# Routing by five-number records instead of finished rows, in a graph and mixture-of-experts kernel

## The chip, the cores and the metric

One core of one Trainium2 chip runs the whole kernel. The metric is device time in microseconds from start to end. Lower is better.

## The reference, cut to what matters

N = 12500 nodes with D = 256 features, 212500 edges, 8 experts with hidden width 512, two experts per node:

```
xn = layernorm(x)
x1 = x + gnn(xn, src, dst, edge_weight) + mix(xn)      # edges: weighted sum of neighbours; mix: gated linear attention
x2 = layernorm(x1)
n  = (x2 - mean(x2)) * rsqrt(var(x2) + eps) * gamma + beta
logits = n @ Wr + br;  top two experts per node;  w = softmax of the two logits
out = x1 + sum over the two experts e:  w_e * (gelu(n @ W1[e] + b1[e]) @ W2[e] + b2[e])
```

## The kernel before, in words

Four phases follow each other, with a barrier of all engines between them. Every engine (PE, DVE, ACT, POOL, and SP, which issues loads and stores) has its own program, written out by hand; semaphores order them.

1. **Setup** (`setup_phase`): constants, edge tables, and clearing of the four accumulators `agg`.
2. **Edges** (`edge_phase`): 1664 chunks of 128 edges in 104 groups of 16. PE and DVE make 128 messages, and POOL adds them into one accumulator with an indirect DMA (L818). Beside the edges, `take_steps` slips in the layer norm of x (the first 25 groups, `normal_steps`), the attention context and the mix; SP stores x + mix as `scratch["x1"]` (L667).
3. **Routing** (`route_phase`): 49 pairs of 128-node tiles. SP loads the four accumulators and x + mix four pairs ahead (`DEPTH = 4`). DVE adds accumulators two and two (`add_halves`, L1629), PE sums and turns them (L1773) and multiplies by the GNN weight (L1784), and DVE adds the result to x + mix, which gives x1 (`gather_sums`, L1623); SP stores x1 to `out`. DVE takes mean and variance (`statistics`) and writes the normalised row into `z` (`normalise`, L1655 and L1657), which has 259 numbers: 256 features, node number, first expert, lead of the first logit over the second. PE turns `z`, ACT applies gamma and beta (`features`), PE makes logits (L1806). DVE picks two experts (`route`) and, with counts that PE makes (L1817 to L1824), each copy's place in its expert's region of a table in DRAM (`position`). POOL scatters each row of `z` twice, with four indirect DMAs a pair (`send`, L1597). At the end SP and ACT write 256 blank rows behind each expert's last row (`fill_up`, L1546), and DVE plans 105 blocks of 256 rows (`plan`).

   The order of one pair on DVE is `route(i-2)`, `gather_sums(i)`, `statistics(i)`, `add_halves(i+2)`, `normalise(i)`, `position(i-2)`. On PE it is `turn(i-1)`, `weigh(i+1)`, `rank(i-2)`, `logits(i-1)`, `sum_turned(i+2)`. On ACT it is `features(i-1)`, the square root for i, `sum_out(i+2)`.
4. **Experts** (`expert_phase`): 105 blocks q, two buffers each. SP loads the block's first-layer weights (L1944) and its 256 rows of the table into `zin` (L1950). PE does the first layer (L1979), turns the next block (L1966), does the second layer (L1989); ACT does gamma, beta and gelu. DVE works out the node numbers and each row's share, adds the bias (L2046) and multiplies by the share (L2052). POOL adds the 256 result rows into `out`, which already holds x1, with two indirect DMAs (L2069). Two copies of one node may stand in neighbouring blocks, so POOL waits until the adds of block q-1 have landed before it issues those of block q:

```
for c in range(2):
    if s == 1:
        pool.wait_ge(s_add[0][c], 16 * k + 16)
    elif not first(k):
        pool.wait_ge(s_add[1][c], 16 * k)
```

## Time and profile before

| what | us |
|---|---|
| median of 3 runs (4436.13 to 4442.04) | 4440.78 |
| the profiled execution | 4440.3 |
| its span in the trace | 4438.6 |
| setup, up to the first add of edges | 0 to about 157 |
| edges | to 3260.9 |
| routing, with its end and the barrier | 3261.0 to 3645.8 |
| experts | 3645.8 to 4438.6 |

In the rows further down, a time at the start of a line counts from the span's start. "Idle before" is the time that an engine stood still before an instruction, with what ended it. Two instructions of one kind in a row overlap a little, so what a pair costs its engine is the distance from its start to the start of the next instruction.

### The profile page before, as it was taken

To read this page: it belongs to the slowest core of one execution; us is meant where nothing else is said; L and a number is where in the kernel's file an instruction comes from. 1 tells how busy PE (TensorE), PEld (TensorE's weight loads), DVE (VectorE), ACT (ScalarE), POOL (GpSimd) and SP (SyncE) were. 2 spreads that over 40 slices of the span, in tenths; PEclk is the share of its full clock that TensorE was granted. 3 is DMA by queue.
4 is the path that set the end of the run, shared out by engine and by line. 5 is a ranking of instruction groups with operands and counts; after the bars stand their busy time and mean duration, and the time that the engine had idled before them with its cause. 6 is when DMAs were issued, how large, how long until landed. Compare 5 with 4: busy or idle time off the path is not lost. (4 is left out here: it accounts for less than half of the span.)

```text
span 4438.6 us, 85552 instructions
## 1 busy us (share of the span) xinstructions
PE 3389.3 (76%) x16628; PEld 2802.7 (63%) x16629; DVE 2495.7 (56%) x11386; ACT 1685.6 (38%) x3095; POOL 3111.7 (70%) x2088
## 2 busy tenths in 40 slices
PE   1466666667677677878888888888758859999998
PEld 1355555555565555666666666666557758888887
DVE  3577777665555555666666666666548862222222
ACT  1233333344444443444444444444312224444443
POOL 0488888888888888888888888888855544444444
PEclk7788878788888888888888888888779979999999
DMA  9888888877777777777777777777789965565554
GB/s 380 241 146 155 152 148 147 157 117 118 116 109 115 116 113 114 102 108 108 105 104 107 108 103 105 108 107 102 91 217 296 294 187 143 139 145 141 141 140 114
DMA packets 588869, 638.95 MB, mean 144 GB/s; under 512 B 60524, under 2 KB 553156, under 8 KB 587138
## 3 DMA queue, kind: packets, MB, share of 16 engines
q0 software_dynamic: 279264, 269.84, 48.5%
q1 hardware_dynamic: 262234, 273.19, 20.9%
q10 hardware_dynamic: 47304, 95.18, 5.9%
q8 instruction: 23, 0.38, 0.0%
q14 instruction: 44, 0.36, 0.0%
HBM read 249.82 MB, written 390.09 MB: 144 GB/s over the span
## 5 line engine op out<-in xcount | busy, mean ns | idle before, releaser
L818 POOL DMA_INDIRECT agg<-msg,sidx x1664 | 2585.7, 1554 | 667.5 <-issue 408.7
L1122 PE MATMUL bank<-rows,Cmat 128*128 x3328 | 1025.7, 450 | 166.7 <-ACT msg L1315 140.6
L1315 ACT COPY msg<-bank 128x512 f32<-128x512 f32 x832 | 487.1, 585 | 1486.0 <-DMA agg<-msg,sidx 1209.8
L1122 PEld LDWEIGHTS bank<-rows,Cmat 128*128 128x128 f32 x3328 | 699.1, 224 | 346.7 <-issue 253.8
L873 DVE SCALAR_TENSOR_TENSOR sidx<-seen_sum,trash,srcf 128x4 int32<-128x4 f32 x416 | 92.7, 223 | 1022.8 <-DMA agg<-msg,sidx 1017.6
L2069 POOL DMA_INDIRECT out_dram<-x_y,x_node x210 | 325.7, 1551 | 473.1 <-issue 228.2
L856 DVE TENSOR_SCALAR Emat<-bank,srcf,wtf 128x128 f32<-128x128 f32 x1664 | 564.5, 398 | 0.0
L1106 PEld LDWEIGHTS bank<-Emat,pick 128*128 128x128 f32 x3328 | 518.3, 226 | 41.6 <-issue 17.7
L1106 PE MATMUL bank<-Emat,pick 128*128 128x128 f32 x3328 | 528.7, 311 | 1.6 <-DVE seen L860 1.6
L1097 PE MATMUL bank<-packed,both 128*128 (+1 forms) x416 | 187.3, 451 | 437.9 <-DVE seen L860 427.9
L860 DVE SCALAR_TENSOR_TENSOR seen<-bank,srcf,prior 128x128 f32<-128x128 f32 x1664 | 479.1, 341 | 0.0
L848 DVE TENSOR_SCALAR pick<-iotaf,locf 128x128 f32<-128x128 f32 x1664 | 384.3, 313 | 13.4 <-issue 12.6
L1097 PEld LDWEIGHTS bank<-packed,both 128*128 (+1 forms) x416 | 47.8, 115 | 530.6 <-issue 408.4
L1979 PE MATMUL bank<-x_xf,x_w 128*128 128x256 f32 x1680 | 381.6, 380 | 1.2 <-ACT x_xf L2005 1.2
L1989 PE MATMUL bank<-expert_rows,x_hT 128*128 x1680 | 380.0, 379 | 0.0
L2021 ACT ACTIVATE x_hT<-bank,ffn_b 128x256 f32<-128x256 f32 x420 | 199.2, 474 | 448.0 <-PE bank L1979 448.0
L1979 PEld LDWEIGHTS bank<-x_xf,x_w 128*128 128x128 f32 x1680 | 320.4, 191 | 45.4 <-issue 1.6
L2046 DVE TENSOR_TENSOR x_y<-bank,expert_rows 128x256 f32<-128x256 f32 x210 | 79.4, 419 | 464.1 <-PE bank L1989 464.1
L1989 PEld LDWEIGHTS bank<-expert_rows,x_hT 128*128 128x128 f32 x1680 | 311.1, 190 | 38.0
L1597 POOL DMA_INDIRECT table<-r_z,r_pos x196 | 197.5, 1008 | 174.5 <-DVE r_pos L1707 112.4
L1306 ACT COPY Cmat<-bank 128x512 f32<-128x512 f32 x416 | 245.3, 590 | 186.0 <-PE bank L1106 184.6
L1321 ACT ACT_TABLE_LOAD x148 | 189.9, 1283 | 7.1 <-SPq L630 4.5
(245 smaller groups left out, 4130.6 us busy)
## 6 DMA issues: line engine op xcount, KB each, us to landing
x_w<-in_L_ffn_W_dram SPq DMA_DIRECT2D x105, 512.0 KB, 4.1
agg<-expert_rows ACTq DMA_DIRECT2D x12, 4224.0 KB, 63.3
r_agg<-agg SPq DMA_DIRECT2D x196, 256.0 KB
x_zin<-table SPq DMA_DIRECT2D x105, 259.0 KB, 4.1
window_raw<-in_x_dram SPq DMA_DIRECT2D x208, 128.0 KB, 2.5
agg<-msg,sidx POOLq DMA_INDIRECT x1664
xn_rows<-n_xn ACTq DMA_DIRECT2D x49, 256.0 KB
xn_turned<-n_xnT ACTq DMA_DIRECT2D x49, 256.0 KB
```

What stands on the lines that cost most here:

```text
L818: pool.indirect_dma_start(scratch["agg"][r][:, :], bass.IndirectOffsetOnAxis(ap=sidx[:, j:j + 1], axis=0), msg[:, j % (2 * BATCH), :], Non ...
L848: nc.vector.tensor_scalar(pick[:, b % 2, q, :], edges["iota"][:], locf[:, bass.ds(BATCH * nb + q, 1)], None, ALU.is_equal)
L856: nc.vector.tensor_scalar(Emat[:, b % 2, q, :], B[b % 2][:, q * P:(q + 1) * P], srcf[:, n], wtf[:, n], ALU.is_equal, ALU.mult)
L860: last = nc.vector.scalar_tensor_tensor(out=seen[:, q, :], in0=B[b % 2][:, q * P:(q + 1) * P], scalar=srcf[:, bass.ds(BATCH * nb + q, 1)], ...
L1097: nc.tensor.matmul(B[b % 2][:, :], edges["both"][:, bass.ds(NB * (g % per) + b, 1)].to_broadcast([P, P]), edges["packed"][:, bass.ds(g // ...
L1106: mm = nc.tensor.matmul(C[:, q * P:(q + 1) * P], pick[:, b % 2, q, :], Emat[:, b % 2, q, :], start=True, stop=True)
L1122: mm = nc.tensor.matmul(M[p][:, (q % 2) * D:(q % 2 + 1) * D], Cmat[:, b % 2, q, :], rows[:, bass.ds(slot, 1), :], start=True, stop=True)
L1306: nc.scalar.copy(Cmat[:, b % 2].rearrange("p q c -> p (q c)"), C[:, :]).then_inc(s_Cc, 1)
L1315: nc.scalar.copy(msg[:, at:at + 2, :].rearrange("p q c -> p (q c)"), M[p][:, :]).then_inc(s_msg, 1)
L1979: mm = nc.tensor.matmul(H[c][:, 0:CAP], w1[:, s, a, c * P:(c + 1) * P], xf[:, s, a, :], start=(a == 0), stop=(a == HALF - 1))
L1989: mm = nc.tensor.matmul(Y[s][:, h * D:(h + 1) * D], hT[:, s, c, h * P:(h + 1) * P], w2[:, bass.ds(e * HC + c, 1), :], start=(c == 0 and h ...
L2069: pool.indirect_dma_start(out[:, :], bass.IndirectOffsetOnAxis(ap=node[:, s, c:c + 1], axis=0), y[:, s, c, :], None, bounds_check=N - 1, o ...
```

## The change

- The table holds records of five numbers: node, first expert, lead, mean, 1/deviation. The routing writes no normalised row. POOL scatters records with the same four indirect DMAs a pair.
- PE turns x1 itself, directly after it is summed. The router's gamma, beta and mean are folded into its weights once, ahead of the loop, and 1/deviation scales the logits afterwards.
- x1 is stored to `scratch["x1"]`. `out` is cleared in the edge phase, by 25 DMAs of 512 KB (the last one smaller) from ACT's queue, one in each of the first 25 groups.
- In the expert phase SP loads a block's records three blocks ahead, DVE turns the node numbers into integers (`tell`), POOL gathers the 256 rows of x1 with two indirect DMAs (`gather`), and DVE normalises them one block ahead (`normalise`). The copy of a node that belongs to its first expert also carries x1 (`own`, `xe`), so that the sums in `out` start at zero. Four slots of records and rows take the place of two of `zin`, and the loop runs over four blocks.

```diff
 def edge_phase
+            def blank_out(n):
...
+                    act.dma_start(out[bass.ds(n * BLANK * P, BLANK * P), :].rearrange("(p a) d -> p (a d)", a=BLANK),
+                                  blank).then_inc(s_blankout, 16)
             def normal_steps(n):
-                steps = [(1, lambda u=u: deviations(n, u)) for u in pairs_of(n)]
+                steps = [(1, lambda u=u: deviations(n, u)) for u in pairs_of(n)] + [(8, lambda: blank_out(n))]
 def route_phase, DVE, statistics(i, u)
                 dve.wait_ge(s_st, 3 * i + 1)
+                if not below(i, DEPTH):
+                    for c in range(2):
+                        for m in range(2):
+                            dve.wait_ge(s_sent[c][m], 16 * (i - DEPTH + 1))
                 dve.nop(nofuse=True)
                 for c in range(2):
-                    last = nc.vector.bn_aggr(mv[:, s, c, :], stat[:, c, :])
+                    last = nc.vector.bn_aggr(rec[:, u, c, MEAN:RSTD + 1], stat[:, c, :])
...
-                nc.vector.reciprocal(scl[:, s], std[:, s]).then_inc(s_scl, 1)
-                dve.wait_ge(s_scl, i + 1)
-                if not below(i, DEPTH):
-                    dve.wait_ge(s_T, i - DEPTH + 1)
-                    for c in range(2):
-                        for m in range(2):
-                            dve.wait_ge(s_sent[c][m], 16 * (i - DEPTH + 1))
-                nc.vector.tensor_copy(z[:, u, :, D], nodes[:, bass.ds(2 * i, 2)])
-                for c in range(2):
-                    last = nc.vector.tensor_scalar(z[:, u, c, 0:D], x1[:, s, c, :], mv[:, s, c, 0:1], scl[:, s, c:c + 1],
-                                                   ALU.subtract, ALU.mult)
-                last.then_inc(s_z, 1)
+                nc.vector.reciprocal(rec[:, u, :, RSTD], std[:, s]).then_inc(s_scl, 1)
+                nc.vector.tensor_copy(rec[:, u, :, NODE], nodes[:, bass.ds(2 * i, 2)])
 route(i, u)
-                nc.vector.tensor_tensor(lg[:], logit, br[:].rearrange("p (a e) -> p a e", a=1).to_broadcast([P, 2, NE]),
-                                        ALU.add).then_inc(s_lg, 1)
+                dve.wait_ge(s_scl, i + 1)
+                for c in range(2):
+                    last = nc.vector.scalar_tensor_tensor(out=lg[:, c, :], in0=logit[:, c, :], scalar=rec[:, u, c, RSTD:RSTD + 1],
+                                                          in1=brc[:], op0=ALU.mult, op1=ALU.add)
 PE, turn(i, u); POOL, send
-                pe.wait_ge(s_z, i + 1)
+                pe.wait_ge(s_sum, i + 1)
-                                                z[:, u, c, :], None).then_inc(s_sent[c][m], 16)
+                                                rec[:, u, c, :], None).then_inc(s_sent[c][m], 16)
 def expert_phase, SP
+            def body(k, u):
+                q, s = SLOTS * k + u, u % 2
                 e = expert_of(sp, q)
-                if not first(k):
+                if not below(q, 2):
                     sp.wait_ge(s_H, HC * (q - 1))
                     sp.nop(nofuse=True)
                 sp.dma_start(w1[:, s], ...)
-                sp.dma_start(zin[:, s], scratch["table"][bass.ds(at, CAP), :].rearrange("(a p) d -> p a d", p=P)).then_inc(s_z[s], 16)
+                if not over(q + AHEAD):
+                    if not below(q, 1):
+                        sp.wait_ge(s_share, q)
+                        sp.nop(nofuse=True)
+                    load_records(*ahead(k, u, AHEAD))
 PE, turn
-                pe.wait_ge(s_z[s], 16 * k + 16)
+                pe.wait_ge(s_zn, q + 1)
 DVE
+            def normalise(k, u):
+                q, s = SLOTS * k + u, u % 2
+                dve.wait_ge(s_gat[u], 32 * k + 32)
...
+                for c in range(2):
+                    last = nc.vector.tensor_scalar(zn[:, s, c, :], xg[:, u, c, :], rec[:, u, c, MEAN:MEAN + 1],
+                                                   rec[:, u, c, RSTD:RSTD + 1], ALU.subtract, ALU.mult)
...
+                    last = nc.vector.tensor_scalar(xe[:, s, c, :], xg[:, u, c, :], own[:, s, c:c + 1], None, ALU.mult)
...
-                    nc.vector.tensor_scalar(y[:, s, c, :], y[:, s, c, :], share[:, s, c:c + 1], None,
-                                            ALU.mult).then_inc(s_y, 1)
+                    nc.vector.scalar_tensor_tensor(out=y[:, s, c, :], in0=y[:, s, c, :], scalar=share[:, s, c:c + 1],
+                                                   in1=xe[:, s, c, :], op0=ALU.mult, op1=ALU.add).then_inc(s_y, 1)
+            def body(k, u):
+                if not over(q + 1):
+                    normalise(*ahead(k, u, 1))
+                if not over(q + AHEAD):
+                    tell(*ahead(k, u, AHEAD))
+                shares(k, u)
+                finish(k, u)
 POOL
+            def gather(k, u):
+                pool.wait_ge(s_row, SLOTS * k + u + 1)
...
+                    pool.indirect_dma_start(xg[:, u, c, :], None, scratch["x1"][0:NPAD, :],
+                                            bass.IndirectOffsetOnAxis(ap=rows[:, u, c:c + 1], axis=0)).then_inc(s_gat[u], 16)
+            def body(k, u):
+                if not over(q + AHEAD):
+                    gather(*ahead(k, u, AHEAD))
```

DVE in the loop of the routing, from the square root's result to the logits, before (`r_std` comes from ACT, `r_sent` counts landed scatters, `r_place`, `run` and `r_pos` belong to `position`, `r_lg` to the next pair's `route`):

```order
L1629 TENSOR_TENSOR r_agg<-r_agg 128x1024 [waits r_sums_loaded0]
L1648 RECIPROCAL r_scl<-r_std 128x2 [waits r_std]
L1654 REGISTER_ALU [waits r_turned,r_scale]
L1655 ISA [waits r_sent10,r_sent11,r_sent01,r_sent00]
L1655 COPY r_z<-nodes 128x2
L1657 TENSOR_SCALAR r_z<-r_x,r_mv,r_scl 128x256 x2
L1695 TENSOR_TENSOR r_place<-bank,run 128x16 [waits r_ranks]
```

The same place with the change, from the statistics on:

```order
L1667 REGISTER_ALU [waits r_stat_step]
L1670 BN_AGGR r_record<-r_stat 128x2 [waits r_sent11,r_sent10,r_sent00,r_sent01]
L1670 BN_AGGR r_record<-r_stat 128x2
L1672 REGISTER_ALU
L1673 TENSOR_SCALAR r_vs<-r_record 128x2 [waits r_stat_step]
L1653 ISA
L1655 TENSOR_TENSOR r_agg<-r_agg 128x1024 [waits r_sums_loaded0]
L1678 RECIPROCAL r_record<-r_std 128x2 [waits r_std]
L1679 ISA
L1679 COPY r_record<-nodes 128x2
L1718 TENSOR_TENSOR r_place<-bank,run 128x16 [waits r_ranks]
```

The two writes of the normalised rows are gone, and the wait for the scatters of four pairs ago has moved from behind the reciprocal to the statistics, about 2 us earlier in the round.

POOL in the loop of the experts, one block before (`x_added` counts landed adds, `x_out_weighted` finished result rows):

```order
L2067 ISA [waits x_added10,x_added11]
L2069 DMA out_dram<-x_y,x_node 12500x256 [waits x_out_weighted]
L2067 REGISTER_ALU
L2069 DMA out_dram<-x_y,x_node 12500x256 [waits x_out_weighted]
L2062 REGISTER_ALU
```

and one block with the change (`x_rows` are the gathered rows, the first of the two names in `x_rows<-x_rows` being the buffer and the second x1 in DRAM):

```order
L2148 DMA x_rows<-x_rows,x_row 128x256 [waits x_rows_told]
L2148 DMA x_rows<-x_rows,x_row 128x256
L2157 ISA
L2160 ISA [waits x_added10,x_added11]
L2162 DMA out_dram<-x_y,x_node 12500x256 [waits x_out_weighted]
L2160 REGISTER_ALU
L2162 DMA out_dram<-x_y,x_node 12500x256 [waits x_out_weighted]
```

Two gathers stand between the adds of one block and the wait for them that precedes the next block's adds.

## Rows read from the trace of the kernel before

**Rows 1.** Stretches: length, PE, PEld, DVE, ACT, POOL busy, PE clock, DMA share, GB/s.

```profile
500.00:700.00 200.00, 134.50 (x611) 109.50 (x611) 147.99 (x675) 62.08 (x130) 167.22 (x108) 0.80 0.85 147
3450.00:3550.00 100.00, 83.11 (x647) 74.30 (x647) 83.63 (x396) 24.68 (x58) 56.44 (x57) 0.95 0.94 294
3664.00:4424.00 760.00, 760.00 (x3725) 669.46 (x3724) 202.79 (x832) 309.72 (x725) 321.04 (x207) 1.00 0.58 140
```

**Rows 2.** A round of routing, DVE and first scatter, timeline: start, duration, instruction.

```profile
3452.16 0.25 DVE L1640 BATCH_NORM_AGGREGATE r_mv<-r_stat 128x2 f32<-128x6 f32 x2
...
3454.25 0.17 DVE L1655 COPY r_z<-nodes 128x2 f32 x1 [0.41 <-DVE r_scl L1648]
3454.33 0.83 DVE L1657 TENSOR_SCALAR r_z<-r_x,r_mv,r_scl 128x256 f32<-128x256 f32 x2
3455.08 0.24 DVE L1695 TENSOR_TENSOR r_place<-bank,run 128x16 f32<-128x16 f32 x2
...
3455.87 0.17 DVE L1707 CAST r_pos<-r_posf 128x4 int32<-128x4 f32 x1
...
3456.90 0.96 POOL L1597 DMA_INDIRECT table<-r_z,r_pos  x1 [2.15 <-DVE r_pos L1707]
```

**Rows 3.** The same round on PE, by the timeline.

```profile
3453.83 2.05 PE L1773 MATMUL bank<-ident,r_agg 128*128 128x128 f32 x16 [0.92 <-DVE r_agg L1629]
...
3458.71 1.04 PE L1806 MATMUL bank<-ffn_wrt,r_xf 128*128 128x8 f32 x8
```

**Rows 4.** Instructions of tile r_x: ns min/median/max, first and last start.

```profile
L1623 DVE TENSOR_TENSOR r_x<-r_xin,bank x49: 686/686/689, 3275.1 to 3611.3; 128x512 f32<-128x512 f32 x49
```

**Rows 5.** Instructions of tile table, the scatters of the routing, and their landing.

```profile
L1597 POOL DMA_INDIRECT table<-r_z,r_pos x196: 957/963/1998, 3292.0 to 3632.8; - x196
...
DMA to landing us min/median/max: 2.9/4.2/8.9
```

**Rows 6.** The end of the routing and the start of the experts, by the timeline.

```profile
3632.82 0.96 POOL L1597 DMA_INDIRECT table<-r_z,r_pos  x1 [1.97 <-DMA table<-r_z,r_pos]
...
3647.78 0.40 SPq L1950 DMA_DIRECT2D x_zin<-table  x1
...
3651.79 1.12 PE L1966 MATMUL bank<-ident,x_zin 128*128 128x128 f32 x4 [30.37 <-DMA x_zin<-table]
```

**Rows 7.** Source line of the barrier behind the routing.

```profile
L1462 POOLq DRAIN  x1: 7084/7084/7084, 3638.6 to 3638.6; - x1
```

**Rows 8.** Adds of the experts on POOL, by the timeline.

```profile
3740.18 1.55 POOL L2069 DMA_INDIRECT out_dram<-x_y,x_node  x1 [3.71 <-DMA out_dram<-x_y,x_node]
3742.04 1.55 POOL L2069 DMA_INDIRECT out_dram<-x_y,x_node  x1 [0.30 <-issue]
3747.83 1.55 POOL L2069 DMA_INDIRECT out_dram<-x_y,x_node  x1 [4.24 <-issue]
...
3754.95 1.55 POOL L2069 DMA_INDIRECT out_dram<-x_y,x_node  x1 [3.72 <-DMA out_dram<-x_y,x_node]
```

**Rows 9.** The adds of the experts (L2069): start to landing, min/median/max.

```profile
DMA to landing us min/median/max: 2.7/4.9/6.2
```

**Rows 10.** One block of the experts on PE and DVE, by the timeline.

```profile
3670.70 3.62 PE L1979 MATMUL bank<-x_xf,x_w 128*128 128x256 f32 x16
3671.03 0.75 DVE L2046 TENSOR_TENSOR x_y<-bank,expert_rows 128x256 f32<-128x256 f32 x2 [5.27 <-PE bank L1989]
3671.82 0.62 DVE L2052 TENSOR_SCALAR x_y<-x_y,x_share 128x256 f32<-128x256 f32 x2
...
3674.16 0.60 PE L1966 MATMUL bank<-ident,x_zin 128*128 128x128 f32 x4
...
3678.05 3.62 PE L1979 MATMUL bank<-x_xf,x_w 128*128 128x256 f32 x16
```

**Rows 11.** Edges: the adds (L818) and DVE's `pick` (L848), by source and tile, 300:3200.

```profile
L818 POOL DMA_INDIRECT agg<-msg,sidx x1558: 1545/1547/1968, 298.9 to 3200.0; - x195
L848 DVE TENSOR_SCALAR pick<-iotaf,locf x1556: 176/281/608, 304.2 to 3194.3; 128x128 f32<-128x128 f32 x195
```

More of the change, by code:

```diff
@@ L54 @@
 ROW = D + 3
+REC = 5
+NODE, FIRST, LEAD, MEAN, RSTD = range(REC)
 TABLE_ROWS = NE * REGION + CAP
@@ L1981, in body @@
                     mm.then_inc(s_H, 1)
-                if not (isinstance(k, int) and q == BLOCKS - 1):
-                    turn(*((k, 1) if s == 0 else (k + 1, 0)))
-                if not first(k):
+                if not over(q + 1):
+                    turn(q + 1, 1 - s)
+                if not below(q, 2):
                     pe.wait_ge(s_yb, q - 1)
@@ L2071, in body @@
                                             compute_op=ALU.add).then_inc(s_add[s][c], 16)
+            for u in range(AHEAD):
+                gather(0, u)
             over_blocks(pool, body)
```

227 lines of the change are left out of this document (140 added, 87 removed).

## The prediction, with its working

> **What bounds the kernel now.** I read the table by stretches first, then one round of each phase in the timeline.
>
> In the edges POOL is the bound: the adds start on average (3200.0 - 298.9) / 1557 = 1.863 us apart, and one takes 1.545 us plus 0.30 us of issue, 1.845 us [rows 8, 11]. Only 0.02 us an add is left for everything else, although the DMA engines are 85% busy [rows 1].
>
> In the routing DVE is. One pair is one round; the 49 sums of x1 start (3611.3 - 3275.1) / 48 = 7.00 us apart [rows 4]. In the round shown DVE stands still only 0.41 us [rows 2]. PE needs from 3453.83 to 3459.75, 5.92 us, for what it does between one sum of accumulators and the next [rows 3], and idles for the rest. POOL needs 4 x (0.96 + 0.30) = 5.04 us. The DMA engines are busy 94% [rows 1], so about 6.6 us of the 7.0, yet no load is what DVE waits for.
>
> In the experts PE is busy 760.00 of 760.00 us at full clock [rows 1]; a block takes 7.35 us [rows 10]. POOL's adds are close behind: three blocks' first adds start 7.65 and 7.12 us apart, 7.39 on average [rows 8]. A block's adds wait for landings, not for results: the result rows of the block before 3674 are ready about 3672.4 [rows 10], while idle times of 3.71 to 4.24 us before the adds end with landings [rows 8].
>
> **The change part by part.**
>
> *Edges.* 25 more DMAs, 12.8 MB in all, go to ACT's queue in the first 25 groups. If no other work hid them, 12.8 MB at the 294 GB/s of the routing [rows 1] are 44 us; that is the upper end. The lower end is 0. I take +1 us: POOL's issue is what counts here, an add has 7.4 us (four adds' spacing) until its accumulator is wanted again, and landings of such adds in the experts have a median of 4.9 us [rows 9]. The cover is POOL's descriptor work; if it were gone, the bytes would show.
>
> *Routing, the round.* DVE loses the two writes of normalised rows, from 3454.33 to 3455.08, 0.75 us, and the stand of 0.41 us ahead of them [rows 2]. The logits are scaled and biased in two instructions where one did it; the pair at 3455.08 takes 0.24 us [rows 2], so against one such instruction 0.1 us more. 7.00 - 0.75 - 0.41 + 0.10 = 5.94 us. PE's 5.92 us stay as they are, since it turns as many tiles; ACT only gets shorter. With both engines at 5.9 and each waiting for the other twice a round I take 6.05 us: 48 x (7.00 - 6.05) = **46 us gained**. POOL's 5.04 us fit. For the DMA engines a pair moves 1.5 MB in place of 2.05, which takes their 6.6 us to about 5. Ends: 5.85 us a round (the last products of PE overlap the next sum), 55 us; 6.4 us, 29 us.
>
> What is late next: the wait for the scatters of four pairs ago, now ahead of the statistics. In the new round it lies 2 T - 2.7 us behind the positions of that pair (two rounds, less the 3.71 us from statistics to positions without the 1.16 us that went, plus 0.17 us of the cast) [rows 2]. The positions, ready at 3456.04, release the first scatter at 3456.90, 0.9 us later [rows 2]; the fourth starts 3.8 us later, and it lands 4.2 us after that at the median [rows 5]: 8.9 us, against 9.4 us at T = 6.05. It fits by half a microsecond.
>
> *Routing, set-up and end.* The folding of weights (four small DVE instructions, eight products, three more) lies in the first microseconds, in which DVE has only the first loads to wait for; +0. At the end the blank rows are 5 KB in place of 259 KB for each of nine DMAs. The last scatter waited 1.97 us where others wait 0.30 [rows 6], and POOL was released at 3638.6 [rows 7], 5.8 us after that scatter's start, where the shortest landing is 2.9 us [rows 5]. Both together give up to 4.6 us; I take **-4**. Then POOL's sequencer drains for 7.1 us [rows 7]. I can't tell from the trace what for, and leave it; that is up to 6 us of downside in the range.
>
> *Experts, the start.* Before, the rows' load is issued at 3647.78 and PE turns them at 3651.79, 4.0 us [rows 6]. Now a chain stands there: records load (between 2.7 and 4.0 us, take 3.3), cast 0.3, first gather 0.3, second gather 1.26 behind it, its landing (2.7 to 6.2 us, take 4.2) [rows 5, 9], normalisation 0.8: 10.2 us, begun about 1 us earlier, by estimate, because no weights load is ahead of it. **+5 us**; ends +3 and +8.
>
> *Experts, the blocks.* PE's work is the same, so 0 as long as nobody makes it wait. The first cover is DVE's: PE turns the next block at 3674.16 [rows 10]. DVE gets the block's products at 3671.03, adds the bias until 3671.82, then weighs and adds x1 (0.62 before; by the pair of 0.75 in rows 2 at most that), then normalises, 0.75: ready about 3673.4, 0.7 us early. DVE's total rises from 202.79 / 760 of 7.35 = 2.0 us a block by about 1.9, to 4. The second cover is POOL's: two gathers of 0.96 + 0.30 = 2.5 us fall into its idle 3.71 to 4.24 us [rows 8]. A gather is not in this trace; its ends are the plain scatter's 0.96 and the add's 1.55 us, and it is a plain copy, so I take 0.96. Even at 1.55 both need 3.7 us and just fit. Should this cover go, every microsecond beyond costs 105 times. SP now waits for a block's shares between two weight loads, but the weights are loaded two blocks ahead; +0. The records' bytes are few, and 256 gathered rows replace 256 loaded ones.
>
> The Trainium skill speaks against this part: "SBUF — State Buffer", section "Who interferes with whom", says that a DVE instruction in a two-port mode, which tensor_scalar on SBUF operands can enter, locks GpSimd out of the port through which it writes descriptors. Four such instructions of 256 columns a block are new here. The trace doesn't agree: beside 1556 `pick` instructions of that form, of 281 ns, the edges' adds take 1547 ns at the median and 1545 at least [rows 11]. By the rule the blocks would be longer; by the rows they are not, and the sum keeps 0. That case is rival B.
>
> **The sum:** -46 - 4 + 5 + 1 = -44 us. 4440.3 - 44 = **4396 us**. The profiled execution's 4440.3 is within 0.5 us of the median 4440.78, so it stands for the median too.
>
> **The rivals.**
>
> *A. The records land too late.* The wait of half a microsecond's spare binds the round: 2 T - 2.7 = 4.7 + landing. With landings of 5.9 us, T = 6.65, a gain of 17 us and 4440 - 17 - 4 + 5 + 1 = **4425**; at 6.6 us T is 7.0 and nothing is left. For: DVE waited at just this wait before, with more time to spare, and landings reach 8.9 us [rows 2, 5]. Against: the engines get a quarter less to move. The Trainium skill ("DMA: Bandwidth & Descriptors", the specifications at its head) says that transfers below 512 bytes are a read-modify-write; the records have 20 bytes. No row here shows a price for it.
>
> *B. The adds become the bound of the experts, and the kernel slower.* The adds' round of 7.39 us is 1.85 us from first to second add and 5.54 us from there to the next block's first, most of it the landing [rows 8, 9]. PE's is 7.35. If gathers in the same queue, or DVE's new instructions, lengthen it, blocks follow it once the lead of some 3 us is used up. From 0.42 us a block on, the whole gain is gone (44 / 105), from 0.5 us the kernel is slower by over 0.2%. Landings longer by 0.8 us give 44 fewer microseconds gained and 80 lost, 4396 + 80 = **4476**. If each of DVE's new instructions from SBUF to SBUF held POOL up for its whole length, the net 0.9 us a block (two pairs of 0.75 less the 0.62 that the weighing took) would give 4396 + 90 = **4486**; that is what the Trainium skill's page "SBUF — State Buffer" would have. For: there is no spare in the chain. Against: the load of 259 KB that now runs at the same time as the adds goes, and landings go down to 2.7 us when loads are absent [rows 9].
>
> *C. The clearing of the output shows.* Half of its bytes on the path are 22 us: **4418**. Against: rows 11.
>
> *D. Better than the sum.* Rounds of 5.85 us, and a shorter drain: 55 + 8 - 4 = 59 us, **4381**.
>
> **How the numbers follow.** Forecast 0.62, A 0.14, B 0.12, C 0.04, D 0.08. 0.2% of the time, 9 us, is about what a measurement of this kernel can tell from no change. Faster by more than that: the forecast, D, nearly all of A and C and a little of B, 0.84. Within it: ends of A, B and C, 0.06. Slower: most of B, 0.10. The range 4376 to 4428 takes in the forecast's ends (rounds of 5.85 to 6.4 us, start +3 to +8, end 0 to -10), D, the middle of A, and C; it leaves out B and the far end of A.
>
> **What would show each step.** Right: sums of x1 about 6.0 us apart with DVE and PE both nearly full; statistics that don't wait for scatters; scatters at 0.96 us; blocks at 7.35 us with PE without gaps; gathers near 0.96 us; the first turn of the experts 9 to 11 us after the first record load; adds of the edges still 1.86 us apart. Wrong: the mean-and-variance instruction waiting for record landings (A); adds in the experts 7.8 us or more apart and PE waiting for the normalised rows (B); adds waiting for landings in the first 25 groups (C).

## The result, and the profile after

| | before | after |
|---|---|---|
| time, median (lowest to highest), us | 4439.55 (4436.13 to 4442.04), 4 runs | 4525.01 (4522.28 to 4529.99), 4 runs |
| ratio to before | | 1.0194, 95% interval 1.0177 to 1.0212 |
| span of the profiled execution, us | 4438.6 | 4528.2 |
| first sum of x1 in the routing | 3275.1 | 3269.1 |
| last sum of x1 | 3611.3 | 3608.5 |
| first add of the experts | 3665.7 | 3663.0 |
| last add of the experts | 4431.0 | 4524.2 |

The change made the kernel slower by 1.9%. The forecast was 4396 us, with a range to 4428: the sign was wrong. The stages say where: up to the first sum of x1 -6.0 us, the 48 rounds of the routing +3.2 (where -46 were forecast), from there to the first add of the experts +0.1, from the first to the last add +95.9 (where 0 was forecast), behind the last add -3.6. Together +89.6 us, the difference of the spans.

The first and the last of these terms lie outside the routing's rounds and the experts' blocks. The -6.0 us do not belong to the change: on another chip the first sums of x1 start at 3273.7 us before it (run before_again) and at 3274.3 us with it (after_again). The -3.6 us are the last drain of POOL's sequencer (source L1888 before, L1915 after), which no term of the forecast has:

```profile
L1888 POOLq DRAIN  x1: 8788/8788/8788, 4429.5 to 4429.5; - x1
```

```profile
L1915 POOLq DRAIN  x1: 5216/5216/5216, 4522.7 to 4522.7; - x1
```

It takes 5.2 us in every run in which POOL gathers among the experts, and 8.8 us in the two kernels that don't (the kernel before and the run x_load).

The stretches of the changed kernel, as in [rows 1] (length, PE, PEld, DVE, ACT, POOL busy, PE clock, DMA share, GB/s):

```profile
500.00:700.00 200.00, 135.50 (x610) 112.34 (x618) 147.66 (x679) 62.92 (x132) 167.05 (x109) 0.81 0.87 167
3450.00:3550.00 100.00, 83.39 (x629) 75.14 (x629) 74.53 (x376) 18.24 (x42) 62.67 (x56) 0.91 0.81 220
3661.00:4421.00 760.00, 702.45 (x3320) 585.51 (x3319) 348.58 (x1288) 278.72 (x645) 482.34 (x365) 1.00 0.57 125
```

In the routing DVE has lost 9 us of work in 100, as intended, and stands still for as much longer. In the experts PE, 760.00 of 760.00 before, is down to 702.45: somebody makes it wait. The rows of the edges (source L825 and L855, 300:3200; [rows 11] before) show nothing of the clearing; the add is even 5 ns shorter, and in the 25 groups with the clearing the adds start 1.86 us apart before and after:

```profile
L825 POOL DMA_INDIRECT agg<-msg,sidx x1562: 1541/1542/1990, 299.1 to 3199.8; - x196
L855 DVE TENSOR_SCALAR pick<-iotaf,locf x1560: 174/282/610, 304.4 to 3194.1; 128x128 f32<-128x128 f32 x195
```

**The routing.** The sums of x1 (tile r_x), the statistics (source L1670) with what ended DVE's idle time ahead of them, and the scatters (source L1612); [rows 2, 4, 5] before:

```profile
L1649 DVE TENSOR_TENSOR r_x<-r_xin,bank x49: 686/689/690, 3269.1 to 3608.5; 128x512 f32<-128x512 f32 x49
...
L1670 DVE BATCH_NORM_AGGREGATE r_record<-r_stat x98: 148/166/185, 3270.7 to 3610.2; 128x2 f32<-128x6 f32 x98
...
  DMA expert_records<-r_record,r_pos: 45.0, 32
...
L1612 POOL DMA_INDIRECT expert_records<-r_record,r_pos x196: 952/958/1974, 3285.9 to 3628.8; - x196
```

(3608.5 - 3269.1) / 48 = 7.07 us a round. The wait that the prediction named as "late next" is there, 32 times, 45.0 us. One of the longer instances, by the timeline:

```profile
3445.59 0.17 DVE L1730 CAST r_pos<-r_posf 128x4 int32<-128x4 f32 x1
3446.62 0.95 POOL L1612 DMA_INDIRECT expert_records<-r_record,r_pos  x1 [1.05 <-DVE r_pos L1730]
...
3450.41 1.46 POOL L1612 DMA_INDIRECT expert_records<-r_record,r_pos  x1 [0.30 <-issue]
...
3457.37 0.25 DVE L1670 BATCH_NORM_AGGREGATE r_record<-r_stat 128x2 f32<-128x6 f32 x2 [2.07 <-DMA expert_records<-r_record,r_pos]
3457.93 1.97 POOL L1612 DMA_INDIRECT expert_records<-r_record,r_pos  x1 [1.53 <-DMA expert_records<-r_record,r_pos]
```

The pair's fourth scatter starts at 3450.41, 4.8 us behind its positions as forecast, but by its semaphore's events it lands at 3457.15, 6.8 us after its start where the working took 4.2. Over the 49 pairs, by the same events (a few per cent of them are missing), the last landing of the four comes 5.6 us after the fourth's start at the median (2.1 to 8.6), and 5.5 us in the kernel before.

The 4.2 us were not a landing of these scatters at all. The line "DMA to landing us min/median/max: 2.9/4.2/8.9" in [rows 5] counts only DMAs on the table whose landing is known, and none of the 196 scatters is among them: they are 105 loads of the experts' rows (source L1950: 3.7/4.1/5.6), 8 stores of blank rows (L1546: 4.2/6.5/8.9) and one more (L1879: 2.9).

**The experts.** Two blocks on POOL, SP (its DMA queue, SPq) and DVE:

```profile
3870.00 1.61 POOL L2162 DMA_INDIRECT out_dram<-x_y,x_node  x1 [1.09 <-issue]
3870.71 0.33 SPq L1986 DMA_DIRECT2D x_record<-expert_records  x1
3871.91 1.65 POOL L2162 DMA_INDIRECT out_dram<-x_y,x_node  x1 [0.30 <-issue]
3872.30 0.39 SPq L1995 DMA_DIRECT2D x_w<-in_L_ffn_W_dram  x1
3873.87 1.01 POOL L2148 DMA_INDIRECT x_rows<-x_rows,x_row  x1 [0.30 <-DMA out_dram<-x_y,x_node]
3875.19 0.99 POOL L2148 DMA_INDIRECT x_rows<-x_rows,x_row  x1 [0.30 <-issue]
3877.34 0.17 DVE L2102 CAST x_node<-x_record 128x2 int32<-128x2 f32 x1 [4.28 <-DMA out_dram<-x_y,x_node]
3878.21 1.63 POOL L2162 DMA_INDIRECT out_dram<-x_y,x_node  x1 [2.03 <-issue]
3880.15 1.68 POOL L2162 DMA_INDIRECT out_dram<-x_y,x_node  x1 [0.30 <-issue]
3880.20 0.38 SPq L1995 DMA_DIRECT2D x_w<-in_L_ffn_W_dram  x1
3881.09 0.66 PE L2017 MATMUL bank<-ident,x_normal 128*128 128x128 f32 x4 [0.57 <-DVE x_normal L2091]
```

The first adds of two blocks are 8.21 us apart; over the stage (4524.2 - 3663.0) / 104.5 = 8.24, against (4431.0 - 3665.7) / 104.5 = 7.32 before (104 distances between first adds, and the last block's second add). From the second add to the next block's first it is 6.30 us here against 5.79 in [rows 8]; over the 96 blocks in mid-stage 6.41 against 5.49. By the landing events the second add lands 3.72 us after its end, against 2.93; the rest of the growth is in the adds themselves, whose second takes 1.68 us where it took 1.55 (medians). The first add lands sooner than before, 3.9 us after its start against 5.6, but the chain waits for the second. PE's idle time is ahead of the turn, behind the normalised rows: DVE normalises the next block only when it is through with the one before, and for that it waits for landed adds (L2102). So everything follows the adds' chain. The gathers last what they were forecast to last, and POOL has room for them.

What SP's queue waits for in the experts, before (3665:4430) and after (3665:4520), by the table of waits:

```profile
SPq L1943 <- PE bank L1979: 449.0, 102, 4.8
```

```profile
SPq L1999 <- DVE x_share L2108: 570.1, 99, 6.4
SPq L2007 <- DMA out_dram<-x_y,x_node: 21.0, 1, 21.0
SPq L1994 <- PE bank L2030: 6.3, 1, 6.3
```

Before, the load of W1 was released by PE. Now its own wait (L1994) ends at once: SP has already been held at the shares (L1999), which DVE works out when adds have landed. So W1, 512 KB, is issued 2.04 us after a block's first add on average, where it was 0.28 us (both from the starts of L1995 and L2162, and of L1944 and L2069, over 96 blocks). By the DMA engines' packets its bytes now move from 3 to 6.5 us after the first add, just when the second add's should (in x_gate below they start at 4 us), and those start at 5 us.

The start of the experts, by the timeline, and the barrier behind the routing (source L1478):

```profile
L1478 POOLq DRAIN  x1: 7084/7084/7084, 3631.2 to 3631.2; - x1
```

```profile
3639.28 2.57 SPq L1986 DMA_DIRECT2D x_record<-expert_records  x3
...
3648.54 1.11 PE L2017 MATMUL bank<-ident,x_normal 128*128 128x128 f32 x4 [30.28 <-DVE x_normal L2091]
```

### The profile page after: what moved, and what is told of

Same layout as the page of the kernel before. It is cut to its first block and busy times, and to the rows that moved or that the text cites. A ratio compares the mean times of both kernels' runs of the same rounds, so it can differ in the third digit from the quotient of the medians.

```text
span 4528.2 us, 86264 instructions
## 1 busy us (share of the span) xinstructions
PE 3396.8 (75%) x16480; PEld 2800.9 (62%) x16637; DVE 2662.7 (59%) x11974; ACT 1665.9 (37%) x3046; POOL 3350.3 (74%) x2298
## 5 line engine op out<-in xcount | busy, mean ns | idle before, releaser
L825 POOL DMA_INDIRECT agg<-msg,sidx x1664 | 2577.2, 1549 | 668.2 <-issue 403.6
L2162 POOL DMA_INDIRECT out_dram<-x_y,x_node x210 | 346.0, 1648 | 262.5 <-issue 241.0
L855 DVE TENSOR_SCALAR pick<-iotaf,locf 128x128 f32<-128x128 f32 x1664 | 385.2, 314 | 14.0 <-issue 13.7
L1104 PE MATMUL bank<-packed,both 128*128 (+1 forms) x260 | 118.0, 454 | 339.8 <-DVE seen L867 329.9
L1612 POOL DMA_INDIRECT expert_records<-r_record,r_pos x196 | 215.1, 1098 | 161.0 <-DVE r_pos L1730 82.2
L2102 DVE CAST x_node<-x_record 128x2 int32<-128x2 f32 x105 | 18.0, 171 | 435.8 <-DMA out_dram<-x_y,x_node 434.5
L2148 POOL DMA_INDIRECT x_rows<-x_rows,x_row x210 | 209.5, 998 | 78.0 <-issue 46.0
```

The source lines that it names most:

```text
L825: pool.indirect_dma_start(scratch["agg"][r][:, :], bass.IndirectOffsetOnAxis(ap=sidx[:, j:j + 1], axis=0), msg[:, j % (2 * BATCH), :], Non ...
L855: nc.vector.tensor_scalar(pick[:, b % 2, q, :], edges["iota"][:], locf[:, bass.ds(BATCH * nb + q, 1)], None, ALU.is_equal)
L2148: pool.indirect_dma_start(xg[:, u, c, :], None, scratch["x1"][0:NPAD, :], bass.IndirectOffsetOnAxis(ap=rows[:, u, c:c + 1], axis=0)).then_ ...
L2162: pool.indirect_dma_start(out[:, :], bass.IndirectOffsetOnAxis(ap=node[:, s, c:c + 1], axis=0), y[:, s, c, :], None, bounds_check=N - 1, o ...
```

## The experiments

The runs of one set share a chip, and chips differ: the kernel before takes 4438 to 4453 us on them, and the changed kernel's routing code, unedited, runs in rounds of 6.9 to 7.5 us. So ratios are to the kernel before on the same chip, and rounds are compared within a set. Even there one code's mean round varies from profile to profile: r_both and all_three have the same routing and differ by 0.24 us. "Round" is the mean distance of the routing's sums of x1, "block" that of the experts' blocks, both from one profile. A ratio without an interval is from one run of each kernel, or of the experiment.

| set | run | ratio | round | block |
|---|---|---|---|---|
| 1 | r_late | 1.021 | 7.34 | 8.22 |
| 1 | x_load | 1.031 | 7.34 | 8.61 |
| 1 | x_narrow | 1.021 | 7.46 | 8.23 |
| 1 | x_relax | 1.000 | 7.40 | 7.32 |
| 2 | r_rank | 1.018 | 7.13 | 8.23 |
| 2 | r_both | 1.018 | 7.09 | 8.23 |
| 2 | x_once | 1.000 | 7.38 | 7.32 |
| 2 | all_three | 0.9994 (0.9984 to 1.0003) | 7.33 | 7.32 |
| 3 | before_again | 1.000 | 7.16 | 7.33 |
| 3 | after_again | 1.0207 (1.0190 to 1.0224) | 7.28 | 8.22 |
| 3 | r_third | 1.023 | 7.46 | 8.21 |
| 3 | x_ahead | 1.017 | 7.19 | 8.05 |
| 4 | x_gate | 0.997 | 6.88 | 7.32 |
| 4 | r_light | 1.018 | 6.95 | 8.22 |
| 4 | r_both_light | 1.016 | 6.60 | 8.25 |
| 4 | gate_both | 0.9946 (0.9929 to 0.9963) | 6.63 | 7.32 |

Runs x_... touch the experts, runs r_... the routing, all_three and gate_both touch both; all edits are made to the changed kernel. x_load, x_narrow, x_once, r_light and r_both_light leave out or replace a part of the work, so their output is not the kernel's; they serve for timing alone.

### Is it the gathers?

x_narrow gathers 64 numbers in place of a row's 256, a quarter of the bytes (NARROW is 64):

```diff
-                    pool.indirect_dma_start(xg[:, u, c, :], None, scratch["x1"][0:NPAD, :],
+                    pool.indirect_dma_start(xg[:, u, c, 0:NARROW], None, scratch["x1"][0:NPAD, :].rearrange("n (a d) -> (n a) d", d=NARROW),
```

> The changed kernel with gathers of 64 numbers of each row in place of 256 (the rest of a row is zero, so the experts' rows are not the right ones). If the adds land late because the gathers' descriptors are written and queued behind them, nothing changes: landing 3.7 us, round 8.3, time about 4525. If it is the gathers' bytes on the DMA engines, landing falls to 3.0 to 3.2 us, round to 7.6, time about 4450.

Block 8.23, nothing changed. The gathers' bytes are not it. x_load has no gathers at all:

```diff
-                    gather(*ahead(k, u, AHEAD))
+                sp.dma_start(xg[:, u], scratch["x1"][bass.ds(64 * (SLOTS * k + u), CAP), :]...).then_inc(s_gat[u], 16)
```

> The changed kernel with the rows of x1 brought by one plain load of 256 rows by SP, in order of rows and not by the records (so the rows that the experts work on are not the right ones), and no gathers on POOL. Theory G (gathers on POOL's queue right behind the adds make the adds land later): landing of the second add after its end falls from 3.7 to about 2.9 us, round of adds from 8.34 to 7.35 to 7.5, time 4435 to 4445. Rival P (the new work of DVE slows the adds themselves and that decides): add's duration stays at 1.63 to 1.68 us, landing stays at 3.7, round about 8.2, time 4510. Rival D (DVE's order, with shares behind normalise and tell, decides): round stays at 8.3.

All three theories missed: the block grew, to 8.61. The gathers are gone and it got worse, so their being gone does not bring the time back; x_once below clears them in full. What came in their place is one more load that SP issues at about the same time as W1, and the second add is further from the next block's first, 6.85 us against 6.41. That pointed to SP's loads.

### Is it the chain of adds, and what lengthens it?

x_relax: the plan adds a tile that holds 16 where the expert changes and 0 elsewhere, and POOL waits by it.

```diff
-                for c in range(2):
-                    if not below(q, 1):
-                        pool.wait_ge(s_add[1 - s][c], 16 * (2 * k + u // 2) + 16 * s)
+                if not below(q, 1):
+                    want = 16 * (2 * k + u // 2) + 16 * s
+                    if not isinstance(k, int):
+                        new = pool.value_load(fresh[0:1, bass.ds(q, 1)], min_val=0, max_val=16)
+                        want = want - 16 + new
+                    for c in range(2):
+                        pool.wait_ge(s_add[1 - s][c], want)
```

> The changed kernel, in which the adds of a block wait for those of the block before only where the expert changes (two blocks of one expert share no node); the adds of two blocks before are still waited for by DVE. Theory: the chain of adds alone makes the round of 8.34 us; without it the experts are bound by PE at 7.35 us again, or DVE's chain at 7.4 to 7.6, time 4430 to 4450. Rival D (DVE's wait for the adds of two blocks before, then shares and finish in one row, is a cycle of its own): round 7.9 to 8.3, time 4480 to 4525.

Block 7.32, as before the change: without the chain of adds the whole loss is gone, and DVE's own order has no cycle that binds. This run alone doesn't say what lengthened the chain, since W1's load moved too: its packets now run 5 to 7.5 us after the first add.

x_once loads W1 for two blocks only:

```diff
-                if not below(q, 2):
-                    sp.wait_ge(s_H, HC * (q - 1))
-                    sp.nop(nofuse=True)
-                sp.dma_start(w1[:, s], ...
+                if below(q, 2):
+                    sp.dma_start(w1[:, s], ...
```

> The changed kernel with W1 loaded for the first two blocks only (all blocks use those weights, so the experts work with the wrong ones), gathers and adds as they are. Theory C (W1's packets, which in the changed kernel run at 3 to 6.5 us of the round of adds, hold up those of the second add): its landing after its end falls from 3.72 to 2.2 to 2.9 us, round of adds from 8.34 to 7.3 to 7.5, ratio to the kernel before 0.995 to 1.003. Rival G (the gathers behind the adds on POOL's queue hold them up, whatever their bytes): landing stays at 3.5 or more, round at 8.1 or more, ratio 1.014 or more.

Block 7.32, with the wait for the block before, the gathers and DVE's new instructions all in place. PE is full again (3700:4400):

```profile
3700.00:4400.00 700.00, 700.00 (x3432) 616.56 (x3431) 343.29 (x1333) 278.55 (x665) 498.53 (x382) 1.00 0.44 71
```

So the chain carries the loss, and W1's load in it makes it. Is it the load's bytes, which were there before the change too, or its time? x_ahead gives W1 four slots, loads a block ahead, and puts the load in front of the records':

```diff
+                if not below(q, 1):
+                    sp.wait_ge(s_share, q)
...
+                if not below(q, 3):
+                    sp.wait_ge(s_H, HC * (q - 2))
...
+                if not over(q + 1):
+                    load_w1(*ahead(k, u, 1))
                 if not over(q + AHEAD):
                     load_records(*ahead(k, u, AHEAD))
```

> The changed kernel with four slots for W1, its load issued one block ahead and in front of the records' load on SP; nothing is left out. Theory C (it is the time at which W1's packets run against those of the second add that costs): they now start up to 2 us earlier in the round of adds, the second add's landing falls from 3.72 to 2.9 to 3.3 us and the block from 8.24 to 7.35 to 7.8, ratio to the kernel before 1.000 to 1.010. Rival (any W1 load beside the adds costs the same wherever it lies, as the bytes are the same): block stays at 8.1 or more, ratio 1.015 or more.

Block 8.05 on average, outside both forecasts, but the average hides two kinds. Two stretches of the same run:

```profile
3905.12 1.61 POOL L2167 DMA_INDIRECT out_dram<-x_y,x_node  x1 [1.21 <-issue]
3906.45 0.37 SPq L1991 DMA_DIRECT2D x_w<-in_L_ffn_W_dram  x1
3907.03 1.59 POOL L2167 DMA_INDIRECT out_dram<-x_y,x_node  x1 [0.30 <-issue]
3912.63 1.62 POOL L2167 DMA_INDIRECT out_dram<-x_y,x_node  x1 [1.39 <-issue]
...
4012.19 1.62 POOL L2167 DMA_INDIRECT out_dram<-x_y,x_node  x1 [2.31 <-issue]
4014.11 1.57 POOL L2167 DMA_INDIRECT out_dram<-x_y,x_node  x1 [0.30 <-issue]
4014.56 0.27 SPq L1991 DMA_DIRECT2D x_w<-in_L_ffn_W_dram  x1
4020.67 1.61 POOL L2167 DMA_INDIRECT out_dram<-x_y,x_node  x1 [2.37 <-issue]
```

Where W1 is issued 1.33 us after the first add, the next block's comes after 7.51 us; where it is 2.37 us, after 8.48. Over 96 blocks: issue before 1.75 us, 25 blocks of 7.5 us; from 2 us on, 53 blocks of 8.4. The 18 blocks between take 8.2 us. The bytes are the same. x_gate takes the step to its end and lets SP issue the load when the adds of three blocks before have landed:

```diff
+                def landed():
+                    if not below(q, 3):
+                        for c in range(2):
+                            sp.wait_ge(s_add[1 - u % 2][c], 16 * (2 * k + (u - 1) // 2))
+                            sp.nop(nofuse=True)
...
+                if not over(q + 1):
+                    load_w1(*ahead(k, u, 1), landed)
+                if not below(q, 1):
+                    sp.wait_ge(s_share, q)
...
```

> As x_ahead, with W1's load issued by SP right when the adds of three blocks before have landed, ahead of its wait for the shares; nothing is left out, and the wait of the adds for the block before stays. In x_ahead the blocks whose W1 load was issued under 1.75 us after the first add took 7.5 us and the others 8.2 to 8.4. Theory C (the time of W1's packets, not their bytes): the issue now falls near the first add's start (within 0.5 us, as in the kernel before, where it is 0.28 us after it), landing of the second add about 2.9 us, block 7.35 to 7.55, ratio to the kernel before 1.000 to 1.007. Rival (the bytes beside the adds cost the same wherever they lie): block 8.1 or more, ratio 1.015 or more.

```profile
3901.85 0.38 SPq L1993 DMA_DIRECT2D x_w<-in_L_ffn_W_dram  x1
3903.29 1.65 POOL L2176 DMA_INDIRECT out_dram<-x_y,x_node  x1 [1.20 <-DVE x_y L2139]
3905.25 1.57 POOL L2176 DMA_INDIRECT out_dram<-x_y,x_node  x1 [0.30 <-issue]
3907.12 1.01 POOL L2162 DMA_INDIRECT x_rows<-x_rows,x_row  x1 [0.30 <-issue]
...
3910.64 1.67 POOL L2176 DMA_INDIRECT out_dram<-x_y,x_node  x1 [1.22 <-DVE x_y L2139]
```

Block 7.32, and a ratio of 0.997, a little better than the forecast of 1.000 to 1.007. The load is issued 1.4 us ahead of the first add, earlier than I had written, the second add lands 2.2 us after its end where 2.9 was expected, and the chain has slack: the first add waits for its result rows (x_y), no longer for landings. The gathers, DVE's new instructions, the load's bytes and the wait for the block before are all still there. Time, not bytes, is shown.

### Why did the routing gain nothing?

r_late keeps mean and 1/sigma in tiles of their own (mv) and copies them into the record two rounds later, behind the wait:

```diff
-                if not below(i, DEPTH):
-                    ... dve.wait_ge(s_sent[c][m], 16 * (i - DEPTH + 1))
-                    last = nc.vector.bn_aggr(rec[:, u, c, MEAN:RSTD + 1], stat[:, c, :])
+                    last = nc.vector.bn_aggr(mv[:, u, c, :], stat[:, c, :])
 route, of the pair two rounds back
+                    ... dve.wait_ge(s_sent[c][m], 16 * (i - DEPTH + 1))
+                nc.vector.tensor_copy(rec[:, u, :, MEAN:RSTD + 1], mv[:, u])
```

> The changed kernel, with mean and 1/sigma kept in a ring of their own and copied into the record two rounds later, so that a slot of records waits for scatters six rounds back, not four. Theory W (the wait at the statistics for the scatters of four pairs before sets the round of 7.07 us): the wait goes from DVE's statistics, rounds fall to 6.1 to 6.4 us, 49 rounds give 33 to 45 us, time about 4480 to 4492. Rival L (the round is bound by loads, turns or the scatters' own chain of four, and the wait only shows it): rounds stay at 6.9 to 7.1 us and the idle time moves to another wait, time 4518 to 4530. Experts' rounds stay at 8.3 us by both.

Round 7.34, within those of untouched routing in the same set (7.34 to 7.46). The wait at the statistics is gone, and in about every second round DVE's position waits for PE's ranks instead (L1721, second row):

```profile
3475.30 0.23 DVE L1721 TENSOR_TENSOR r_place<-bank,run 128x16 f32<-128x16 f32 x2
3483.16 0.26 DVE L1721 TENSOR_TENSOR r_place<-bank,run 128x16 f32<-128x16 f32 x2 [1.37 <-PE bank L1857]
```

A new bound right behind the old. r_rank lifts that one alone, r_both lifts both:

```diff
-                    weigh(i + 1, (u + 1) % DEPTH)
                 if not below(i, 2):
                     rank(i - 2, (u - 2) % DEPTH)
+                if not (isinstance(i, int) and i == PAIRS - 1):
+                    weigh(i + 1, (u + 1) % DEPTH)
```

> The changed kernel, with PE's rank sums of a pair put ahead of the weighing of the next, not behind it. Theory two bounds (the wait for the scatters at the statistics, and behind it a cycle of two rounds in which DVE's position waits for the ranks that PE works out behind the weighing): this edit alone lifts the second only, so rounds stay at 7.1 to 7.4 us and time within 15 us of the changed kernel's (ratio to the kernel before 1.016 to 1.020). Rival (PE's order alone was the bound, and the wait at the statistics was slack): rounds fall to 6.1 to 6.6, ratio 1.008 to 1.012.

> Both edits of the routing together: the late record and the rank sums ahead of the weighing. Theory two bounds: neither wait is left, rounds fall to DVE's own row of 6.3 to 6.6 us, ratio to the kernel before 1.008 to 1.012. Rival (loads at four fifths of the DMA engines, or PE at its lower clock, bound the round whatever the order): rounds stay at 7.1 or more, ratio 1.016 or more.

7.13 and 7.09, against 7.38 in x_once, whose routing is untouched. That is 0.25 to 0.29 us, hardly more than the 0.24 us by which r_both's routing differs from itself in all_three; r_both stands where its rival said (7.1 us, ratio 1.016 or more), not at the forecast 6.3 to 6.6. r_third has the late record and the ranks ahead too, moves the logits ahead of the weighing, turns a pair in its own round instead of the next, and moves ACT's copy to fit:

> The routing with the late record, and PE's round in the order ranks, logits, weighing, turning (of the same pair), sum, with ACT's copy of the turned rows moved to fit: DVE then finds ranks and logits done a stage earlier. Theory (a row of bounds that lie close together: the scatters' wait, the ranks, the logits, each hidden by the one before it; the last is DVE's own row): no wait of DVE on PE is left, rounds fall to 6.4 to 6.7 us, about 0.4 us under those of r_both, ratio to the kernel before 1.010 to 1.015. Rival (PE, at 5.5 us of matmuls of a round at full clock and more at the lower one, is the bound): rounds stay at 7.0 or more.

7.46, no gain: DVE now waits for ACT's square root, which stands in ACT's queue behind a copy that waits for PE. This run can't tell how near PE is. all_three has r_both's routing and x_relax's experts:

> The changed kernel with both edits of the routing and with adds that wait for the block before only where the expert changes. If the gains of the routing (20 to 45 us) and of the experts (about 95 us) add up: ratio to the kernel before 0.988 to 0.996. If the routing's edits bring nothing: 0.999 to 1.001.

The routing brought nothing here (7.33; the ratio 0.9994 is from ten runs), so its second forecast held. Three of its rounds as stretches, with the columns of the first table by stretches above (the granted clock is third from the end):

```profile
3349.79:3359.33 9.54, 5.70 (x52) 5.17 (x53) 5.71 (x29) 0.20 (x1) 6.48 (x8) 1.00 0.81 228
3359.33:3369.41 10.08, 7.71 (x37) 6.90 (x35) 5.68 (x29) 1.20 (x3) 4.56 (x5) 0.54 0.57 166
...
3376.50:3383.77 7.27, 5.77 (x47) 4.90 (x46) 5.73 (x29) 2.11 (x5) 3.22 (x4) 1.00 0.66 162
```

Most rounds take 6.5 to 7.4 us at full clock, and eight take 8.8 to 10.5; the longest stand at or next to a stretch in which the granted clock is 0.54 to 0.83, PE partly at 1.2 GHz; ahead of the fall shown it was busy 5.70 of 9.54 us. Whether PE counts apart from that was asked by leaving out half of its sum (`for r in range(1)`), without and with the two repairs:

> The changed kernel with half of PE's sum of the edges' rows in the routing left out (8 of 16 products a round; the output lacks half of the edges' sums). Theory W first (the scatters' wait at the statistics bounds the changed kernel's round, PE does not): rounds stay at 7.1 to 7.3 us. Rival (PE with its falls to the lower clock is the bound throughout): rounds fall by 0.6 us or more, to 6.7 or less.

> The late record and the rank sums ahead, with the same half of PE's sum left out. If PE is what is left as bound once the scatters' wait is gone: rounds fall from 7.09 to 6.5 to 6.7 us, DVE's own row. If DVE, its loop or something else is the bound: rounds stay at 6.9 to 7.1.

6.95 against 6.88 in x_gate (untouched routing, same chip), and 6.60 against 6.63 in gate_both (both repairs). The 6.95 meets neither of its forecasts, 7.1 to 7.3 and 6.7 or less, as this chip's rounds are shorter anyway; it is the comparison on one chip that counts. The 6.60 lies in the range that was forecast for PE as the bound, but gate_both, with PE's whole work, lies there too: PE's amount of work doesn't bound the round on this chip, the order of waits does. The repairs give 0.25 us a round here, and 0.35 between the two light runs. Not every round gets shorter: the short ones go from 6.2 to 6.5 us, while of the nine rounds over 7.6 us in x_gate (up to 11.1) one is left in gate_both (8.35). Why the long ones go is not shown. What is left is DVE's own row; three rounds of 6.5 and one of 7.3, the loop's turn, repeat in gate_both:

> The changed kernel with the late record, the rank sums ahead and the gated W1 load, nothing left out. If both repairs hold: blocks of 7.35 to 7.55 us and routing of 7.1 us, ratio to the kernel before 0.996 to 1.004; if the gate fails, 1.015 or more.

```profile
L1650 DVE TENSOR_TENSOR r_x<-r_xin,bank x49: 686/689/690, 3271.5 to 3589.6; 128x512 f32<-128x512 f32 x49
```

(3589.6 - 3271.5) / 48 = 6.63. With nothing left out gate_both is 0.5% faster than the kernel before, on one chip, better than the forecast 0.996 to 1.004, and by the two ratios (0.9946 / 1.0207, from two chips) 2.6% faster than the changed one: the best of all.

The two unedited kernels on one chip, for reference:

> The kernel before, unedited, so that its stages can be read on the chip that the other runs are on. Expected: routing in rounds of 7.0 us, blocks of 7.32 us as in the first trace; if this chip is slower by its own nature, it shows in the edges' stage or evenly in all.

> The changed kernel, unedited, for the same reason. Expected: ratio to the kernel before 1.017 to 1.022, routing in rounds of 7.3 to 7.45 us (as in the runs with untouched routing), blocks of 8.23 us.

Ratios and blocks are as expected; the rounds are 7.16 us for the kernel before (7.0 expected) and 7.28 for the changed one (7.3 to 7.45). The two kernels' routings are 0.07 to 0.12 us apart in both pairs of profiles: the change gained nothing there.

## Why the prediction was wrong

**Experts' blocks, forecast 0, came to +96 us.** The step that failed is the sentence "SP now waits for a block's shares between two weight loads, but the weights are loaded two blocks ahead; +0." I asked only whether PE would get its weights in time. It did, nearly (PE's weight loads waited for it 25 times, 7.3 us in all, and its matmuls 4 times, 1.2 us). I didn't ask what else the load meets when its time is set by another event: it became tied to the adds' landing and fell on the second add in every block, +0.92 us x 104.5. In mid-stage, where the growth is 0.98 us a block, 0.8 us of it are the later landing and some 0.2 us are the adds' own, longer beside DVE's new instructions. The kernel before issues the same 512 KB at another point of the round and runs at PE's pace (x_gate, x_once).

**Rival B had the place and the size, and not the cause.** Its chain of adds without spare and the 0.8 us of later landing are what happened; the 0.8 us were an example without a working, so that the size fits is luck. It named gathers in the queue or DVE's new instructions as what would lengthen the chain, and its 4476 us took the routing's 46 us as gained; without them 4440 + 80 + 5 - 4 + 1 = 4522, against 4525 measured. x_narrow, x_once and x_gate clear the gathers. In x_once and x_gate DVE's instructions are all there and the block is 7.32, so they don't bind by themselves; once the chain binds they add the 0.2 us above. The chance of 0.12 was too low: that the load of 259 KB goes spoke for shorter landings, and I let it outweigh that the two rounds, 7.39 and 7.35 us, were equal to start with.

**Routing, forecast -46, came to +3.** The term "7.00 - 0.75 - 0.41 + 0.10 = 5.94" treated DVE's row as the bound. Three things failed. The 8.9 us from positions to the last landing was too short. Its landing of 4.2 us was read off a line that counts none of the scatters, and the round waits for the last of four: 5.6 us behind the fourth's start at the median, 6.8 in the instance shown. That is rival A (its "landings reach 8.9 us" is a blank row's), whose formula gives (4.7 + 5.6 + 2.7) / 2 = 6.5 with the median and 7.1 with 6.8; 7.07 was measured, so the long landings and the other waits make up the rest. Part of the lateness is POOL's: 38 of the 196 scatters take over 1.1 us beside DVE's sum (below), where 0.96 was forecast for all. Behind it stood another bound, which I hadn't listed: PE's ranks come behind the weighing, and DVE's position needs them 1.2 us earlier now that two writes ahead of it are gone. And DVE's own row is not 5.94 but some 6.3 (the shortest rounds of x_gate are 6.2, 6.2 and 6.8 in turn); that the loop's turn and the added waits make the difference is my reading, not shown. With the first two lifted, 48 x 0.25 = 12 us come back on the chip of set 4, in the profiles and in the times (gate_both 4414.7 us, x_gate 4424.6; r_both_light 4506.8, r_light 4518.6). On the chip of set 2 r_both's profile has as much, but ten runs of all_three have nothing, so there no gain is shown.

**What held.** Edges: +1 forecast, nothing to be seen of the clearing (rival C is out). End of the routing: -4 forecast; the drain begins 2.4 us after the last scatter against 5.8 us before [rows 6, 7], -3.4, and takes 7.1 us still. The "shortest landing" of 2.9 us in that working is also not a scatter's, so the size was partly luck. Start of the experts: 9 to 11 us from the first load of records to the first turn forecast, 3648.54 - 3639.28 = 9.3 measured; with the earlier start it costs nothing net. Gathers: 0.96 us forecast, 0.99 measured. The rule on DVE and GpSimd is taken up below. Whether a record of 20 bytes is slower to land than a row of 1 KB, no run tells: by the semaphores' events the scatters land 4.4 us after their start at the median with both, but the DMA engines are busy 0.81 of the time with the records and 0.94 with the rows.

## What to carry to other kernels

When a load's wait changes from one event to another, its time within the round changes too: write down which transfers it will now meet, and whether a chain hangs on those, even if its own consumer has a block to spare. Where two cycles of a loop are equal within 1%, a change that touches both needs a price for each, and "0" is not a neutral guess. Work taken off the fullest engine is worth only the distance to the next cycle through waits; take from the timeline each wait that ended just in time, and use the last of a set of landings, not the median of one. When a view of a tensor gives one figure for several kinds of DMA, look up which of them it counts.

## What the runs showed of the hardware

A load of SP's queue that comes first holds up POOL's adds. In the kernel before, W1's packets run from about 1.5 to 4 us after the first add, and the adds' first packets come at 3.9 us (medians over mid-stage); in x_gate, where W1's run from 0.3 to 2 us, they come at 2.2 us, as in x_once, which has no W1. In the changed kernel it is the second add's that are late: 3.2 us after its start, against 2.15 in x_gate and x_once. (Before, the load of 259 KB was there as well, from 3 to 5.5 us, so that case is not W1's alone.) The Trainium skill ("DMA: Bandwidth & Descriptors", section "SWDGE vs HWDGE vs iDMA") says that the two kinds feed different internal queues of an engine, between which it takes turns. The trace doesn't show equal turns: before, all of W1's packets have started when the adds' first one does, and in the changed kernel most of them.

DVE's instructions do lengthen POOL's DMA instructions. The adds of the experts take 1.55 us before and 1.61 to 1.68 beside the new instructions on SBUF operands. In the routing it hangs on which starts first. In the changed kernel 66 of the 196 scatters run beside DVE's sum of 128x1024, which takes 1.22 us. Of the 42 that start after the sum (by 0.08 us or more), all but the one that meets its last 0.1 us are longer than 0.96 us, up to 1.97, and end about 0.84 us after the sum does; the 24 others start at most 0.03 us after the sum, most of them before it, and take 0.95 to 0.97 us. In the kernel before, 64 run beside the sum, 24 of them start behind it, mostly near its end, and 11 take over 1.1 us. By the Trainium skill ("SBUF — State Buffer", section "Who interferes with whom") a DVE instruction with two operands in SBUF contends with GpSimd's reads: the scatters agree where the sum comes first, and the sum's 1.22 us bounds what they lose. For the adds the price is a tenth of a microsecond each, not the instruction's length, so the 4486 us that the prediction worked out from the page were not reached by that way.
